# Attention sums on TensorE by plain products with the identity, the weighted sum held and rescaled in PSUM

## The reference

```python
z = layernorm(x)
q, k, v = z @ Wq + bq, z @ Wk + bk, z @ Wv + bv            # (4096, 8, 64)
scores = einsum('ehd,ehd->eh', q[row], k[col]) / 8 + bias   # per edge and head
p = exp(scores - segment_max(scores, row)[row])
out = segment_sum(p / segment_sum(p, row)[row] * v[col], row)
x1 = x + out @ Wo + bo
ff = silu(layernorm(x1) @ W1 + b1) @ W2 + b2                # 512 -> 1024 -> 512
result = layernorm(x + x1 + ff)
```

## Time and profile before

| | us |
|---|---|
| median of 3 runs | 4988.64 |
| lowest, highest | 4966.76, 5004.79 |
| span of the profiled execution | 4610.2 |

### The profile page before, as it was taken

The page is one execution under the profiler, slowest core; times in us unless marked ns, Lnnn a source line. Parts: engine busy times, 40 slices in busy tenths (PEclk is TensorE's granted clock), DMA queues, the critical chain, the costliest instruction groups (busy, mean ns, idle before and its releaser), DMA issues.

```text
span 4610.2 us, 73226 instructions
## 1 busy us (share of the span) xinstructions
PE 3227.0 (70%) x18717; PEld 2461.0 (53%) x18717; DVE 2862.0 (62%) x6445; ACT 2094.3 (45%) x6748; POOL 3100.7 (67%) x3033
## 2 busy tenths in 40 slices
PE   4576877776877546777677776777777777777766
PEld 3344444444444235666565665656656555656655
DVE  9766666666666335666556665666565565665654
ACT  0011112111111135666566666666566566665664
POOL 0177777777777767777777777777676676666752
PEclk5577766777767668888888888888888888888888
DMA  4233333333334355655666656665665665656542
GB/s 168 66 113 115 107 102 112 109 102 107 112 100 111 102 192 188 208 183 184 222 203 214 214 196 205 221 214 182 213 210 166 210 206 190 203 185 211 189 150 82
DMA packets 282999, 756.58 MB, mean 164 GB/s; under 512 B 92435, under 2 KB 94675, under 8 KB 281862
## 3 DMA queue, kind: packets, MB, share of 16 engines
q0 software_dynamic: 213664, 577.32, 38.1%
q1 hardware_dynamic: 68454, 169.70, 12.1%
HBM read 759.20 MB, written 58.87 MB: 177 GB/s over the span
## 4 chain that ended last, share of the span: by engine, by line
issue 23%; PE 21%; POOL 16%; DVE 14%; DMA 11%; DVEq 9%; ACT 3%; POOLq 1%; ACTq 1%; SPq 0%; PEld 0%; PEldq 0%
POOL records L378 8%; PE bank L1144 7%; DMA records<-rec_w,pos_i 5%; PE bank L1179 5%; POOL region_a L447 5%; DVE region_c L864 4%; PE bank L1227 3%; DMA region_a<-kv,cols 3%; DVEq L990 2%; DMA region_c<-hiT 2%; PE bank L1201 2%; DVEq L792 2%; DVE hi_oh L728 2%; ACT region_a L669 1%; PE bank L1093 1%
## 5 line engine op out<-in xcount | busy, mean ns | idle before, releaser
L447 POOL DMA_INDIRECT region_a<-kv,cols x1160 | 1311.3, 1130 | 449.5 <-issue 342.5
L378 POOL DMA_INDIRECT records<-rec_w,pos_i x1024 | 1046.9, 1022 | 534.3 <-issue 515.1
L669 ACT ACTIVATE region_a<-region_a,pr 128x64 f32<-128x64 f32 x4640 | 1132.5, 338 | 58.5 <-issue 46.6
L1179 PE MATMUL bank<-ident,region_a 128*128 128x128 f32 x4640 | 708.2, 308 | 345.5 <-issue 281.8
L864 DVE TENSOR_TENSOR region_c<-region_a,region_c 128x1024 f32<-128x1024 f32 x580 | 734.4, 1308 | 283.8 <-DMA region_a<-kv,cols 239.4
L1144 PE MATMUL bank<-ident,region_c 128*128 128x128 f32 x4640 | 664.9, 307 | 329.2 <-DVE region_c L864 329.0
L1179 PEld LDWEIGHTS bank<-ident,region_a 128*128 128x128 f32 x4640 | 619.1, 161 | 425.0 <-issue 322.6
L1144 PEld LDWEIGHTS bank<-ident,region_c 128*128 128x128 f32 x4640 | 624.1, 201 | 373.0 <-DVE region_c L864 372.9
L1093 PE MATMUL bank<-region_c 64*128 64x64 f32 x2048 | 346.4, 337 | 204.7 <-issue 178.9
L1093 PEld LDWEIGHTS bank<-region_c 64*128 64x128 f32 x2048 | 327.7, 248 | 293.4 <-issue 259.4
L542 ACT COPY rec_w<-region_a 128x64 f32 x128 | 31.3, 245 | 960.5 <-DMA records<-rec_w,pos_i 960.5
(11 more groups left out here) (147 smaller groups left out, 4264.8 us busy)
## 6 DMA issues: line engine op xcount, KB each, us to landing
region_c<-srcT SPq DMA_DIRECT2D x128, 512.0 KB
region_c<-hiT SPq DMA_DIRECT2D x128, 256.0 KB
region_a<-kv,cols POOLq DMA_INDIRECT x1160, 5.8
records<-rec_w,pos_i POOLq DMA_INDIRECT x1024
kv<-region_c SPq DMA_DIRECT2D x32, 512.0 KB
records<-pad_rec SPq DMA_DIRECT2D x16, 576.0 KB, 16.9
region_a<-in_x_dram SPq DMA_DIRECT2D x32, 256.0 KB
qx<-region_a SPq DMA_DIRECT2D x32, 256.0 KB
```

What stands on the lines that cost most here:

```text
L378: pool.indirect_dma_start(records, bass.IndirectOffsetOnAxis(ap=pos_i[j % 2][:, s:s + 1], axis=0), rec_w[j % 2][:, s, :], None).then_inc(S ...
L447: pool.indirect_dma_start(KV[h][:, s, :], None, kv, bass.IndirectOffsetOnAxis(ap=cols[h][:, s:s + 1].bitcast(I32), axis=0), bounds_check=L ...
L669: last = act.activation(v, v, ACT.Copy, scale=pr[h][:, s, hd:hd + 1])
L1179: last = pe.matmul(vT_ps[:, c * P:(c + 1) * P], KV[h][:, s, C + c * P:C + (c + 1) * P], ident[:, :], start=s == 0 and c == 0, stop=s == GR ...
```

## The change

The score sums become plain products: the identity is the stationary operand, and the moving one is a strided view of `prods` with 4 slots x 8 heads x 8 channels = 256 columns. Eight of them for each half (`BLOCKS` = 8) leave 8 partial sums for each score in PSUM, not turned, and one more product with 32 columns adds the biases to the first of the eight. VectorE reduces the eight in one instruction of 512 elements. The copy `take_scT`, `turn_scores` and `fold` go.

The weighted sum becomes one product of 512 columns for each slot, identity against v, into a PSUM bank `acc_ps` that stays open over all groups of a tile. `take_vT`, `turn_sum`, `add_sum` and `acc` go. VectorE rescales `acc_ps` in PSUM once a group (`scale_acc`), between the exponential and its share of v, after a wait for all pairs of group g-1; TensorE's first pair of g waits for it (`acc_scaled`). The running maximum becomes one more entry of `sc`, so one reduction and one subtraction take the place of two each, and the end of a tile (`finish`) moves ahead of the weighting of v in stage 0. POOL's program and the loops are the same.

```diff
-    SH = SUB * HEADS
-    FOLD = P // SH
+    SH = GROUP * HEADS
+    BLOCKS = D // ADD          # ADD = 8
@@ ScalarE, body
-                    take_scT()
                     norms(stage)
                     act.wait_ge(S["sc_ready"], g + 1)
-                    act.activation(pr[h][:, :, :], sc[h][:, :, :], ACT.Exp).then_inc(S["p_ready"], 1)
-                    ... take_vT()
+                    act.activation(pr[h][:, 0:GROUP + 1, :], sc[h][:, :, :], ACT.Exp).then_inc(S["p_ready"], 1)
@@ VectorE
             def scale_acc(h):
-                dve.tensor_tensor(heads(acc), heads(acc), pr[h][:, GROUP, :]..., ALU.mult)
-                dve.drain()
+                dve.wait_ge(S["summed"], dve.snap(groups) * PAIRS + 2 * PAIRS)
+                dve.tensor_tensor(heads(acc_ps[:, :]), heads(acc_ps[:, :]), pr[h][:, 0, :]..., ALU.mult)
@@ VectorE, body
                     products(h)
-                    if stage > 1:
-                        add_sum()
                     ...
                     dve.wait_ge(S["sc_summed"], g + 1)
-                    dve.tensor_tensor(s_all, sc_ps..., bias_w[h][:, :, :], ALU.add)
+                    dve.tensor_reduce(s_all, sc_ps, AX.X, ALU.add)
                     dve.drain()
-                    dve.tensor_reduce(m_new[:, :], s_all..., AX.X, ALU.max)
-                    dve.drain()
-                    dve.tensor_tensor(m_new[:, :], m_new[:, :], m_run[:, :], ALU.max)
+                    dve.tensor_reduce(m_new, sc[h]..., AX.X, ALU.max)
                     dve.drain()
-                    dve.tensor_tensor(s_all, s_all, m_new..., ALU.subtract)
-                    dve.tensor_tensor(sc[h][:, GROUP, :], m_run[:, :], m_new[:, :], ALU.subtract).then_inc(S["sc_ready"], 1)
-                    dve.drain()
-                    dve.tensor_copy(m_run[:, :], m_new[:, :])
-                    if stage > 0:
-                        scale_acc(1 - h)
+                    dve.tensor_tensor(sc[h][:, :, :], sc[h][:, :, :], m_new..., ALU.subtract).then_inc(S["sc_ready"], 1)
                     late(stage)
+                    if stage == 0: ... add_weights(1 - h), finish() ...
                     dve.wait_ge(S["p_ready"], g + 1)
+                    if stage > 0:
+                        scale_acc(h)
+                        dve.drain().then_inc(S["acc_scaled"], 1)
                     for s0 in range(0, SUB, 2):
                         ...
@@ TensorE
-            prod_cols = prods.rearrange("p s (h j i) -> p i (s h) j", h=HEADS, j=FOLD)
+            prod_sums = prods.rearrange("p s (h b i) -> p b s h i", h=HEADS, i=ADD)
             def sum_d(h, a):
-                for i in range(D // FOLD):
-                    last = pe.matmul(scT_ps[:, a * P:(a + 1) * P], prod_cols[:, i, a * SH:(a + 1) * SH], ident[:, :],
-                                     start=i == 0, stop=i == D // FOLD - 1, is_transpose=True)
+                if a == 0:
+                    pe.wait_ge(S["sc_ready"], n)
+                for b in range(BLOCKS):
+                    pe.matmul(sc_ps[:, of, :, :], ident[:, :], prod_sums[:, b, of, :, :], start=b == 0, stop=False, ...)
+                last = pe.matmul(sc_ps[:, of, :, 0], ident[:, :], bias_w[h][:, of, :], start=False, stop=True, ...)
             def sum_v(h, pair, fresh=False):
-                if pair == 0:
-                    pe.wait_ge(S["vT_sb_ready"], g)
+                if pair == 0 and fresh:
+                    pe.wait_ge(S["att_ready"], t)
+                if pair == 0 and not fresh:
+                    pe.wait_ge(S["acc_scaled"], pe.snap(n_acc) + 1)
                 ...
                 for s in (2 * pair, 2 * pair + 1):
-                    for c in range(KT):
-                        last = pe.matmul(vT_ps[:, c * P:(c + 1) * P], KV[h][:, s, C + c * P:C + (c + 1) * P], ident[:, :],
-                                         start=s == 0 and c == 0, stop=s == GROUP - 1, is_transpose=True, ...)
+                    last = pe.matmul(acc_ps[:, :], ident[:, :], KV[h][:, s, C:2 * C], start=fresh and s == 0, stop=s == GROUP - 1, ...)
@@ TensorE, body
-                    turn_scores()
                     tail(stage, 0)
-                    ... turn_sum()
```

More of the change, by code:

```diff
@@ L34 @@
 SUB = GROUP // 2
+ADD = 8
 STREAMS = 8
@@ L840, in _ @@
             n_resets = dve.alloc_register("dve_resets")
[L841 removed]
+            for r in (groups, n_prods, *loads, n_out, n_resets):
                 dve.reg_mov(r, 0)
```

162 lines of the change are left out of this document (51 added, 111 removed).

## The result

| | before | after |
|---|---|---|
| median of the runs taken together, us | 4977.7 | 5163.5 |
| ratio, with its 95% interval | 1 | 1.038 (1.032 to 1.044) |
| span of the profiled execution, us | 4610.2 | 5154.8 |
| first stage in it (not touched), us | 1639.2 | 1909.3 |
| second stage in it, us | 2971.0 | 3245.5 |

The change makes the kernel 186 us slower by the medians, where the forecast had 309. In a second set of runs, on another chip, the ratio was 1.029 (1.023 to 1.034), 146 us. The time, 5163.5 us, is 134 us under the forecast of 5298 and inside the range.

What follows compares the result with a forecast made beforehand. A ring of dependences bounds the kernel now, TensorE after the change: 2688 us of work plus gaps, clock, waits and ends make 3280 us against 2971, so 309 us on the 4988.64 median gives 5298 us, range 5130 to 5520.

Steps and rivals of the forecast that it cites:

- the bound at 512 columns: Score sums on TensorE: a 256-column product costs at most as much as 512 columns, 14.0 us for the 32 instructions.
- (a): TensorE's gap between tiles: 7.5 us left at each of 31 turns, 232 us.
- (b): TensorE's register read of the number of groups in stage 1: 1.3 us left each time, 40 us.
- (c): TensorE's slow clock after the gap between tiles: 3.6 us at each of 31 turns, 112 us.
- (d): Chain from last score sum to first weighted v: 4.0 us, partly covered by TensorE's other work, 103 us left.
- (e): TensorE's wait for KV at a new tile: 2 us each, 62 us, as TensorE and POOL's path are about level.
- the gaps hide under a full TensorE queue: Rival at tile turns: gaps and slow clock go, waits for KV grow to 350 us; about 5200 us, chance 0.14.
- if the gap between tiles is gone: Sign of being wrong: TensorE's gap between tiles vanishes, where the forecast expected it still at 7 us or more.
- the slack rival: Rival in the second stage: TensorE's idle time absorbs the 943 us, a gain of 180 us to 4809 us, chance 0.07.
- 378 us above the span, which the change does not touch: Base of the forecast: the median of 4988.64 us exceeds the profiled span by 378 us, carried over unchanged.
- Nothing is covered: Rival at tile turns: gaps stay in full and the clock costs its upper bound, 257 us more, 5555 us, chance 0.12.
- Runs of eight: Rival in the score sums: strided runs read slowly, 1018 us more, 6316 us, chance 0.03.

Runs made afterwards that it cites:

- after_extra: Kernel after plus four idle products of 512 columns at the end of each body, 509 us of work in all; ratio 1.097 to the kernel before.
- more_scores: Kernel after with twelve in place of eight blocks of channels in the score sums, 501 us more work; ratio 1.149 to the kernel before.
- half_scores: Kernel after with four of the eight blocks of channels in the score sums, 501 us less work; ratio 0.953 to the kernel before.
- bf16_scores: Kernel after with the products of q and k written as bfloat16 and summed with a bfloat16 identity; 4747 us, ratio 0.956 to the kernel before.
- vsum_only: Kernel before with only the new weighted sum, plain products into PSUM and rescaled there; ratio 1.004 to the kernel before.
- before_extra: Kernel before plus four idle products of 512 columns at the end of each body, 509 us in all; ratio 1.051 to the kernel before.
- scores_only: Kernel before with only the new score sums as plain products; ratio 1.034 to the kernel before.

## Why the prediction was right, and where not

**The direction and TensorE's work: right.** The added work was 14.41 us a group by the forecast; the timeline has 2 x (3.45 + 0.14) + 16 x 0.43 = 14.1 us. The runs of eight elements cost nothing, and the bound at 512 columns was far off. The mechanism that decides is the one named: plain float32 products take the array nearly twice the time, and TensorE becomes the engine that sets it. Between the turns it idles for 6% of the time, work put in there comes back at 83 to 94% (after_extra, more_scores), and work taken out of the score sums is time gained (half_scores, bf16_scores).

**The sum for the second stage: right as a whole, by two errors that cancel.** It gave 3280 us; the two profiles of after have 3246 and 3231. Term by term for the first of them: work 2688; (a) gaps 95 (73 of them at the turns) against 232; (b) register read 30 against 40; (c) above work 108, all of it the low clock (109 by the time at 1.2 GHz), against 112; (d) chain 110 against 103; (e) waits for the products, at new tiles above all, 160 (249.5 less the 89 us wait ahead of the stage's first sums) against 62; the remainder, ends and small waits, 55 against 43.

**(a), the gap between tiles, failed in its count.** The forecast left 7.5 us at each of 31 turns. There were 9 turns with a gap, at 8.1 us on average, all of them at the end of tiles with five or more groups. The rival "the gaps hide under a full TensorE queue" had this and its consequence: without the gap, TensorE comes earlier to the new tile and waits there for the products of its KV. The other 22 turns have such a wait and no gap, 9.8 to 12.5 us in the six out of tiles with five groups and 3.8 to 7.8 us in the fifteen out of tiles with four (11.4 us at the one out of a tile with three); no turn has both over 2.5 us. So (e) rose by 98 of the 137 us that (a) lost: gap and wait take each other's place. That the sum came out near is luck in this sense, as the forecast had 7.5 and 2 us at every turn. Its own sign of being wrong, "if the gap between tiles is gone", came true at 22 of 31 turns.

**How much of the added work disappears: right on the side of after, wrong on that of before.** With 309 us for 943 us of work the forecast let 634 be absorbed. Against the usual execution of before it was 805, as 138 us are left. After the change the forecast had 3280 - 2688 = 592 us beyond the work, and the two profiles have 558 and 543. Before it, it had 2971 - 1745 = 1226, where a usual execution has 1355. Of the 805 us, 507 are idle time (950 against 443): 228 us of turn gaps, and 268 us of waits ahead of `turn_scores` and `turn_sum` (L1154, L1164), which went with the instructions, whatever else TensorE did. The other 298 are busy time above the work (405 against 107). Two thirds of them, 196 us, are the clock: TensorE was busy at 1.2 GHz for 605 us before and for 213 after, and half of that is the cost. The rest is ends of bursts, and 45 us of it the forecast's price of a group. This is what the slack rival described, only not to the end.

**The base was the step that failed: "378 us above the span, which the change does not touch".** Spans of all later profiles are within 3 us of their execution's time, so no 378 us lie around a span there. The forecast added it unchanged to a second stage that it had worked out in absolute terms. Right would have been to ask what a usual execution looks like when span and median are 8% apart: with a first stage of 1909 us (as in the profile after) and its own 3280 us it comes to 5189 us, 26 us from the 5163.5 measured. The effect of 309 us was 1.7 to 2.1 times the measured 186 and 146 for the same reason: the 3280 us are near the usual execution of after, the 2971 are a quick one of before. The terms were read from the quick execution too, so that they fit the usual one of after is partly luck; whether the kernel after has a quick one isn't known. Smaller slips in the working: the 0.114 us an instruction for W1 stands in none of its rows (0.120 by busy time), and "TensorE idles some 1200 of the 2971 us" counts slow instructions as idle, as its idle time was 858.

**What the last part said would show it.** 0.216 and 0.43 us for the two sizes: seen. Busy time up by 900: only 647 (2796 against 2149), as before's clock was low and its bursts were short. POOL's wait for TensorE up from 107 to 376 us (121 and 141 in the usual executions of before): seen. VectorE's wait for the score sums above that for KV: 703 against 139 us, seen. Gaps still at 7 us or more: their mean yes, their number no. `scale_acc` waits "a few tenths at most": seen, 27 us in 61 times. Its 0.7 us on the path, part of term (d), were worth 101 us when cut to a quarter.

**The rivals.** "Slack absorbs it, faster" fell, though vsum_only comes near it (1.004, 450 us of work for 11), and so does the half of the extra work that before_extra absorbs. "The gaps hide" came nearest on mechanism, for 22 of the turns, and its 5200 us lie nearer to the 5163.5 than the forecast's 5298, if on the same wrong base; its second stage of 3184 us is 62 short. "Nothing is covered" fell. "Runs of eight" fell by the pace.

## What to carry to other kernels

Price added work by where it falls, and look for the slack by stretch and not in one share. In the kernel after TensorE is busy for 86% of the second stage, but for 94% between the turns, and there added work cost 83 to 94% of itself, at the end of a body or in the score sums. The same idle products cost 47% in the kernel before, where TensorE idled for 23% of that time. At the turns 109 us of added work vanished, while the longer score sums made the turns 134 us longer. The repairs that gained took work out of the score sums (to VectorE, or by a narrower type); `scores_only`, which has 450 us less work in the weighted sum than the kernel after, is no faster (3252 against 3238 us). Where a profiled span and the median of the runs are some per cent apart, do not carry the difference along as a constant: it may be an unusual execution, and a sum worked out in absolute terms must be set against the usual one. When a gap in one engine's stream and a wait for data lie at the same place, they share their time, so bound the two together and do not add them.

## What the runs showed of the hardware

The pauses of TensorE at the turn of a tile, "issue" in every view, go with the traffic of one DMA queue. The instruction queue q8 of the page in the kernel after, 

```profile
q8 instruction: 111, 1.82, 0.2%
```

and in more_scores, which differs from it only in the trip count of one loop of TensorE's program, written out in full:

```profile
q8 instruction: 283, 4.64, 0.4%
```

(packets, MB, share of the engines). Over all kernels of the table, 24 to 43 turn gaps go with 270 to 285 packets, 8 or 9 with 107 to 111, and 0 to 3 with 75 to 97. The number of TensorE's instructions in the second stage goes the same way: 12932 to 14672 in the first set, 10612 in the second, 8002 or 8292 in the third, with 11772 in after_extra as the exception, which has no gap.

The packets also come at the turns that pause. At the turn of more_scores shown above (4634 to 4652 us) the queue has

```profile
q8 instruction: 6, 0.10, 3.0%
```

as at each of its fifteen turns out of tiles with four groups. In the kernel after, fourteen of those fifteen turns have no packet and one has two, and none has a gap; its nine turns with a gap have 3 to 5 packets each, the six other ones out of tiles with five groups one. It is no fixed pair: after_extra has five turns with 3 packets and no gap, and vsum_only a pause of 6.3 us at a turn without any. This fits a program whose parts are fetched again when it is long, with the pause hidden when enough work is queued. half_scores, after and more_scores differ in that one trip count and have 76, 111 and 283 packets, so the number follows TensorE's program; that the fetch makes the pause was not measured by itself. The Trainium skill, "Advanced Engine Details and Errata", section Engine Queue Depths, gives TensorE a queue of 64 instructions, which bears on how long a pause can be hidden; no run here shows its depth.

The clock followed the load without any change of code: 0.83 and 0.84 in the second stage of before, 0.87 with idle products added, 0.94 and 0.95 after, 0.97 in after_extra. By the time that TensorE was busy at 1.2 GHz, 605 us before and 213 after, it gave back about 196 of the 943 us of added work here.
